# Batch 0's experts chosen in pieces one half of the attention earlier, the last batch's logits and positions moved forward, two batches' shared down products moved behind the experts

## The chip, the core and the metric

The kernel runs on one core of a Trainium2 chip. The metric is the time of one execution in microseconds on the device, as the median of several runs. Engines: PE is TensorE (matmuls; PEld its weight loads), DVE is VectorE, ACT is ScalarE, POOL is GpSimd, SP is SyncE, which here only issues transfers. Each engine runs its own program in order; they wait for each other on semaphores.

## What is computed

One transformer block on x of shape (4, 512, 256): four batches of 512 tokens, model width 256.

```
mod = silu(c) @ wmod -> sa, ca, ga, sb, cb, gb           (per batch; |ga|, |gb| kept >= 0.25)
h   = layernorm(x) * (1 + ca) + sa
att = causal softmax attention(h): 32 query heads, 8 key/value heads, head width 8
x   = x + ga * (att @ wo)
h   = layernorm(x) * (1 + cb) + sb
scores = softmax(h @ gate_w.T)                            (16 experts, 4 groups of 4)
keep the 2 groups with the largest score, then the 4 largest experts in them;
w = their scores, normalised to sum 1
out = sum over experts e of w[e] * (swiglu(h @ expert_up_w[e].T) @ expert_down_w[e].T)
    + swiglu(h @ shared_up_w.T) @ shared_down_w.T
x   = x + gb * out
```

The experts' inner width is 176, that of the shared expert 352.

## The kernel before, in words

**Attention.** It is done in eight halves (u = 0 to 7): batch u // 2, and one half of the heads. A half goes through 10 groups n, each a pair (quarter q of 128 queries, tile kt of 128 keys), and each group through four steps g. A step does one score product into one bank of PSUM (L692, `scores`), which ScalarE exponentiates (L1138); on the diagonal GpSimd masks the result (L1264). Two groups later TensorE multiplies by the values (L703, `weigh_values`), and ScalarE takes the sums out of PSUM (L1119). Meanwhile TensorE computes the scores of the next half a first time, to find the row maxima: 22 pairs of banks in a half (L670, L673, `scores_for_max`), which VectorE reduces (L1456); two pairs of banks exist, so pair n waits for VectorE to be done with pair n - 2. The maxima are transposed (`turn_max`). In the even halves the projection of the batch before (L723, `project`) stands in group 9, and VectorE adds it to x. The score pairs of half 0 are computed before the halves begin (L849), between the projections of q, k and v.

**Bank 7.** The small products of the attention (turned maxima, projections, turned rows, logits, positions) share bank 7; a table, `misc_use` (L290 to L308), numbers them in order, and each waits until the one before is read out.

**The experts' routing,** once for each batch m. VectorE normalises the rows (stats, mean, `centre`) and scales them (`scale_rows`); TensorE transposes them (`turn_first_rows` for batch 0, `turn_rows2` otherwise) and multiplies by the gate (L792, `logits`); VectorE takes the largest logit (L1555) and subtracts it (`begin`); ScalarE exponentiates (`exponential`); VectorE chooses groups and experts (`choose`), some twenty small instructions; TensorE counts, for every row and expert, how many rows come before it (L806 to L812, `positions`); VectorE turns these into slots (`place`, L1594 to L1610); and GpSimd scatters the rows to `x_rows` in memory, 16 indirect DMAs for each batch (L1350), each with 128 rows. GpSimd's program is in order too: the masks of half 7 and the scatters share it.

In the kernel before, batch 0 goes through the logits in half 6 (group 7) and through choose and place in half 7, ahead of VectorE's other work there; batch 1 through its logits in group 5 of half 7; logits(2) stands between the last two value products, before positions(1). GpSimd issues four scatters of batch 0 before the last quarter's masks of half 7, and twelve behind them.

**After attention** come, on TensorE, the shared expert's up products (L879, three parts k for each batch) and down products (L900, two parts h for each batch), the last projection (L916, `project_last`), and between them the routing of batches 2 and 3. Before place(3) SP can't write the 16 pads (L561), which fill the last tile of every expert; behind them it loads the rows tile by tile (L565). The down products of batches 0 to 2 are taken out by ScalarE (L1178) and written to `y_sum[0]`.

**The experts.** 79 tiles of 128 rows: transposed (L953), up (L965), down (L987, L992), weighed by VectorE (L1756), and added into `y_sum` in memory by GpSimd's indirect DMA (L1391). Behind the last tile TensorE computes the down product of batch 3 (L900), which VectorE multiplies by gb and adds to x (L1776, L1779). VectorE adds all parts (L1786 to L1791) after `y_sum` is read back, and the result is written.

The order of the products after attention:

```
shared_up(0, 0); shared_up(0, 1); positions(2); shared_up(0, 2); shared_up(1, 0); shared_up(1, 1)
project_last(0); project_last(1); shared_up(1, 2); shared_up(2, 0); turn_rows2(3)
shared_up(2, 1); logits(3); shared_down(0, 0); shared_down(0, 1); positions(3)
shared_up(2, 2); shared_down(1, 0); shared_down(1, 1); shared_up(3, 0..2); shared_down(2, 0..1)
```

## Time and profile before

| | |
|---|---|
| median of 3 runs | 697.05 us (695.75, 697.05, 705.97) |
| the profiled execution | 700.47 us, of which the span is 698.6 us |
| PE busy | 601.9 us, 86% |
| DVE busy | 403.8 us, 58% |
| ACT busy | 304.6 us, 44% |
| POOL busy | 344.9 us, 49% |
| mean granted clock of TensorE | 0.917 |

The profile comes from one execution. Its span goes from the first to the last recorded instruction; all times in the text are microseconds from its start. Busy time is the time in which at least one instruction of an engine runs; the granted clock is that of TensorE, 1.00 being 2.4 GHz. Half 0 begins at about 72 us, half 7 ends at about 346, the experts run from about 466 to 668.

### The profile page before, as it was taken

What the parts mean: (1) busy time and instruction counts of PE and PEld (TensorE: products, weight loads), DVE (VectorE), ACT (ScalarE), POOL (GpSimd) and SP (SyncE); (2) the same over time, 40 slices, a digit from 0 to 9 for tenths busy, and PEclk for the clock granted to TensorE, in tenths of its full rate; (3) what the DMA queues carried; (4) which work ended last, traced back from release to release, by engine and by line L of the source; (5) the groups of instructions that cost most, each with busy time, mean ns of one, the idle gap of its engine ahead of it and who ended that gap; (6) DMA issues with size and microseconds to landing.
All of it is one profiled execution on the core that took longest, in us unless ns stands there. A gap on an engine that the chain in (4) does not pass through costs nothing.

```text
span 698.6 us, 11637 instructions
## 1 busy us (share of the span) xinstructions
PE 601.9 (86%) x3377; PEld 323.7 (46%) x3377; DVE 403.8 (58%) x819; ACT 304.6 (44%) x626; POOL 344.9 (49%) x451
## 2 busy tenths in 40 slices
PE   7988799999999999998949539939999999999950
PEld 5455433344434443443324116616666666666530
DVE  5668577877898789868744056503333333333327
ACT  2424577776677677757610033113232323323200
POOL 5017745362637273625757702703666666666630
PEclk7989799999999999989969759969999999999975
DMA  9698569674141414201339902544676777777567
GB/s 277 163 274 171 172 138 336 159 218 107 36 107 37 106 37 106 39 17 19 119 95 380 352 37 82 208 127 96 123 124 122 124 130 125 119 127 128 77 124 276
DMA packets 86180, 98.01 MB, mean 140 GB/s; under 512 B 12868, under 2 KB 78964, under 8 KB 85864
## 3 DMA queue, kind: packets, MB, share of 16 engines
q1 hardware_dynamic: 70040, 75.90, 39.2%
q0 software_dynamic: 14448, 19.80, 15.9%
q10 hardware_dynamic: 1632, 1.57, 0.7%
q8 instruction: 30, 0.49, 0.3%
q14 instruction: 30, 0.25, 0.1%
HBM read 50.55 MB, written 43.65 MB: 135 GB/s over the span
## 4 chain that ended last, share of the span: by engine, by line
PE 46%; DMA 18%; issue 11%; DVE 7%; ACT 7%; POOL 5%; SPq 4%; another core or an unknown queue 3%; POOLq 0%; ACTq 0%; DVEq 0%
DMA y_sum<-arena 13%; PE bank L703 9%; PE bank L692 9%; PE bank L965 6%; PE bank L670 4%; ACT arena L1138 4%; PE bank L673 3%; PE bank L987 2%; POOL arena L1264 2%; PE bank L723 2%; ACT arena L1119 2%; PE bank L992 2%; DMA arena<-x_rows 1%; PE bank L623 1%
## 5 line engine op out<-in xcount | busy, mean ns | idle before, releaser
L1456 DVE TENSOR_REDUCE negm<-bank 128x2 f32<-128x1024 f32 (+3 forms) x176 | 192.6, 1121 | 54.9 <-PE bank L673 53.6
L1138 ACT ACTIVATE arena<-bank 128x512 f32<-128x512 f32 x320 | 181.1, 600 | 81.0 <-PE bank L692 74.3
L1391 POOL DMA_INDIRECT y_sum<-arena x79 | 123.1, 1558 | 96.5 <-DVE arena L1756 47.9
L1264 POOL TENSOR_SCALAR_AFFINE_SELECT arena<-arena 128x512 f32<-128x512 f32 x128 | 81.0, 647 | 119.7 <-ACT arena L1138 117.0
L692 PE MATMUL bank<-arena 75*128 75x512 bf16 x320 | 119.6, 394 | 8.8 <-ACT arena L1138 3.0
L965 PE MATMUL bank<-arena 128*128 x316 | 105.9, 478 | 0.6 <-ACT arena L1206 0.3
L1350 POOL DMA_INDIRECT x_rows<-arena,slots x64 | 64.3, 1004 | 55.0 <-DVE slots L1610 36.5
L703 PE MATMUL bank<-arena 128*9 128x512 f32 x640 | 85.6, 607 | 5.3 <-POOL arena L1264 4.1
L1756 DVE TENSOR_SCALAR arena<-bank,arena 128x256 f32<-128x256 f32 x79 | 38.2, 484 | 84.9 <-DMA y_sum<-arena 34.3
L673 PE MATMUL bank<-arena 118*128 118x128 bf16 x512 | 83.8, 228 | 2.4 <-DMA arena<-k_rows 2.4
L670 PE MATMUL bank<-arena 72*128 72x128 bf16 (+2 forms) x384 | 83.4, 279 | 2.6 <-DVE negm L1456 2.6
L1212 ACT ACTIVATE arena<-bank 128x176 f32<-128x176 f32 x79 | 25.1, 318 | 127.3 <-PE bank L965 83.3
L692 PEld LDWEIGHTS bank<-arena 75*128 75x128 bf16 x320 | 30.4, 99 | 98.5 <-ACT arena L1138 82.4
L965 PEld LDWEIGHTS bank<-arena 128*128 128x128 f32 x316 | 57.7, 192 | 39.5 <-issue 15.2
L673 PEld LDWEIGHTS bank<-arena 118*128 118x128 bf16 x512 | 48.2, 102 | 20.5 <-issue 3.6
L879 PE MATMUL bank<-arena 128*128 128x512 f32 (+1 forms) x96 | 49.6, 661 | 8.9 <-issue 8.9
L1748 DVE TENSOR_TENSOR arena<-bank,arena 128x128 f32<-128x128 f32 x79 | 23.1, 292 | 57.3 <-ACT arena L1212 54.3
L670 PEld LDWEIGHTS bank<-arena 72*128 72x128 bf16 x384 | 38.4, 100 | 27.3 <-DVE negm L1456 16.8
L987 PE MATMUL bank<-arena 128*128 x158 | 41.5, 385 | 3.1 <-DVE arena L1756 1.7
L953 PE MATMUL bank<-ident,arena 128*128 128x128 f32 x158 | 25.4, 278 | 13.0 <-DMA arena<-x_rows 12.9
L879 PEld LDWEIGHTS bank<-arena 128*128 128x128 f32 (+1 forms) x96 | 19.0, 202 | 33.9 <-issue 33.8
L1206 ACT ACTIVATE arena<-bank 128x256 f32<-128x256 f32 x79 | 26.6, 382 | 11.2 <-PE bank L953 11.1
(190 smaller groups left out, 704.5 us busy)
## 6 DMA issues: line engine op xcount, KB each, us to landing
arena<-x_rows SPq DMA_DIRECT2D x79, 144.0 KB, 2.5
arena<-q_rows SPq DMA_DIRECT2D x8, 1200.0 KB, 9.2
q_rows<-arena SPq DMA_DIRECT2D x24, 384.0 KB, 4.4
arena<-up_t SPq DMA_DIRECT2D x2, 2816.0 KB
arena<-y_sum SPq DMA_DIRECT2D x8, 512.0 KB, 6.7
x_rows<-arena SPq DMA_DIRECT2D x17, 144.0 KB
k_rows<-arena SPq DMA_DIRECT2D x24, 96.0 KB, 3.2
arena<-k_rows SPq DMA_DIRECT2D x8, 288.0 KB
```

The source lines that it names most:

```text
L670: nc.tensor.matmul(bank[:, buf + j, at_:at_ + n - P], Q[k][0:PR, head, q * P:q * P + P], K[k][0:PR, head // REP, 0:n - P], start=(c == 0), ...
L673: last = nc.tensor.matmul(bank[:, buf + j, at_ + n - P:at_ + n], Q[k][0:MR, head, q * P:q * P + P], K[k][0:MR, head // REP, q * P:q * P + ...
L692: nc.tensor.matmul(bank[:, score_bank(u, tile), :], K[k][0:KR, g, kt * P:kt * P + P], Q[k][0:KR, g * REP:g * REP + REP, q * P:q * P + P], ...
L703: last = nc.tensor.matmul(bank[32 * g:32 * g + VW, OBANK, :], V[:, b * QT + kt, h * GH + g, :], probs[:, (NG * u + n) % SLOTS, g, :], star ...
L879: last = nc.tensor.matmul(bank[0:w, 2 * k + i, :], ws_up[:, c, c0:c0 + w], h2T[n][:, c, :], start=(c == 0), stop=(c == DC - 1))
L965: last = nc.tensor.matmul(bank[:, 2 + t % 2, 0:2 * I], xT[t % 2][:, c, :], w[:, bass.ds(e * (DC * 2 * I) + c * 2 * I, 2 * I)], start=(c == ...
L987: nc.tensor.matmul(bank[:, 6 + i, 0:D], actT[p % 2][:, i, :], main[:, bass.ds(expert[2 * p + i] * D, D)], start=True, stop=False, skip_gro ...
L1138: nc.scalar.activation(probs[:, group % SLOTS, g, :], bank[:, score_bank(u, tile), :], ACT.Exp, scale=SCALE).then_inc(s["st_free"], 1)
L1264: nc.gpsimd.affine_select(out=block_, in_=block_, compare_op=ALU.is_ge, fill=0.0, base=0, pattern=[[0, REP], [1, P]], channel_multiplier=- ...
L1350: gp.indirect_dma_start(x_rows, bass.IndirectOffsetOnAxis(ap=slots[:, t, k:k + 1], axis=0), rows[:, t, :], None).then_inc(s["rows_out"], 16)
L1391: gp.indirect_dma_start(y_sum[t % 2], bass.IndirectOffsetOnAxis(ap=xt[t % XT][:, D:D + 1].bitcast(U32), axis=0), yo[t % YO], None, compute ...
L1456: nc.vector.tensor_reduce(to, view, AX.X, ALU.max, negate=True).then_inc(s["s_free"], 1)
```

## The change

**First half.** Ten products of the identity with itself, whose result nobody reads, stand before half 0, and two more before each of the last four score pairs of half 0. On GpSimd low(3), a small step of the projections, moves from behind the first quarter of half 0 to behind the second.

**Half 6.** The transposes of batch 0 move from groups 4 and 5 to group 2, logits(0) from group 7 to group 4. choose(0) is cut into six pieces, which stand between VectorE's maxima in groups 5 to 7; positions(0) and place(0) follow in group 8. scale_rows(1) moves out of half 6 to the place that choose(0) had in half 7.

**Half 7.** turn_rows2(1) stands in group 1 (was 0), logits(1) in group 3 (was 5), turn_rows2(2) in group 5 (was 7), logits(2) in group 7 (was between the last two value products). GpSimd issues three scatters of batch 0 before the first masks, one behind the second quarter, four behind the third, and the other eight behind the last.

**After attention.** shared_up(2, 1) is cut in two, and logits(3) stands between the parts. positions(3) stands before all four down products of batches 0 and 1 and no longer waits for the first one's eviction. The down products of batch 2 stand behind the experts, with those of batch 3, in banks 0 to 3; VectorE adds both batches' to x, and only batches 0 and 1 go to `y_sum[0]`, which is zeroed for two batches instead of one.

The diff, cut to its core:

```diff
-AMID = 4
+AHEAD, AMID = 3, {1: 1, 2: 4}
...
-                    if u == HALVES - 2 and q == QT - 2:
+                    if u == HALVES - 2 and q == 1:
                         for c in range(DC):
                             misc_use["rows", c] = len(misc_use)
+                    if u == HALVES - 2 and q == 2:
+                        misc_use["logits", 0] = len(misc_use)
...
+        CHOOSE_AT = {(5, 2): 0, (6, 0): 1, (6, 3): 2, (7, 1): 3, (7, 2): 4, (7, 3): 5}
...
-                        sp.dma_start(y_sum[0][(B - 1) * T:NT * P, :].rearrange("(t p) d -> p t d", p=P),
-                                     zeros[:, 0:QT, :]).then_inc(s["y_zero"], 16)
+                        sp.dma_start(y_sum[0][(B - 2) * T:NT * P, :].rearrange("(t p) d -> p t d", p=P),
+                                     zeros[:, 0:2 * QT, :]).then_inc(s["y_zero"], 16)
...
+                    for j in range(idle):
+                        nc.tensor.matmul(bank[:, buf, 0:P], ident[:, :], ident[:, :], start=True, stop=True,
+                                         skip_group_check=True)
...
                             if u == HALVES - 2:
-                                if (n, g) in ((4, 1), (5, 1)):
-                                    turn_first_rows(n - 4)
+                                if (n, g) in ((2, 0), (2, 3)):
+                                    turn_first_rows(g // 3)
+                                if (n, g) == (4, 1):
+                                    logits(0)
+                                if (n, g) == (8, 1):
+                                    positions(0)
+                            if u == HALVES - 1:
+                                if (n, g) == (1, 1):
+                                    turn_rows2(1)
+                                if (n, g) == (3, 1):
+                                    logits(1)
+                                if (n, g) == (5, 1):
+                                    turn_rows2(2)
                                 if (n, g) == (7, 1):
-                                    logits(0)
-                            if u == HALVES - 1:
-                                if (n, g) == (0, 3):
-                                    turn_rows2(1)
-                                if (n, g) == (3, 3):
-                                    positions(0)
-                                if (n, g) == (5, 1):
-                                    logits(1)
-                                if (n, g) == (7, 1):
-                                    turn_rows2(2)
+                                    logits(2)
...
-                        pe.wait_ge(s["ys_ready"], 2)
...
-                        scores_for_max(0, q, i)
+                        scores_for_max(0, q, i, 2 if pair > 17 else 0)
...
+                for i in range(10):
+                    nc.tensor.matmul(bank[:, 3, 0:P], ident[:, :], ident[:, :], start=True, stop=True)
...
                 weigh_values(HALVES - 1, 8)
-                logits(2)
                 weigh_values(HALVES - 1, 9)
                 positions(1)
...
-                    if n == B - 1:
+                    if n == 2:
                         pe.wait_ge(s["xT_ready"], TILES)
+                    if n == 3:
+                        pe.wait_ge(s["a_ready"], TILES)
+                    k_ = 7 - h if n < 2 else 2 * (n - 2) + h
...
-                shared_up(2, 1)
+                shared_up(2, 1, range(1))
                 logits(B - 1)
-                shared_down(0, 0)
-                shared_down(0, 1)
+                shared_up(2, 1, range(1, 2))
+                shared_up(2, 2)
                 positions(B - 1)
-                shared_up(2, 2)
-                shared_down(1, 0)
-                shared_down(1, 1)
+                for n in range(2):
+                    for h in range(2):
+                        shared_down(n, h)
                 for k in range(3):
                     shared_up(3, k)
-                for h in range(2):
-                    shared_down(2, h)
...
-                for h in range(2):
-                    shared_down(B - 1, h)
+                for n in range(2, B):
+                    for h in range(2):
+                        shared_down(n, h)
...
+                EXPONENTIAL_AT = [(HALVES - 2, 5, 0), (HALVES - 1, 4, 3), (HALVES - 1, 9, 1)]
...
+                exponential(B - 1)
                 shared_silu(2, 1)
-                exponential(B - 1)
+                shared_silu(2, 2)
                 store(0)
-                shared_silu(2, 2)
                 store(1)
                 for k in range(3):
                     shared_silu(3, k)
-                store(2)
...
                 for u in range(HALVES):
+                    if u == HALVES - 1:
+                        gp.wait_ge(s["numbered"], 4)
+                        gp.wait_ge(s["routed"], 1)
+                        for k in range(AHEAD):
+                            scatter_first()
...
-                        if (u, q) == (0, 0):
+                        if (u, q) == (0, 1):
                             low(3)
...
-                        if u == HALVES - 1 and q == 2:
+                        if u == HALVES - 1 and q == 1:
                             inverse_deviation(B - 2)
-                            gp.wait_ge(s["numbered"], 4)
-                            gp.wait_ge(s["routed"], 1)
-                            for k in range(AMID):
-                                scatter(0, k)
+                        if u == HALVES - 1 and q in AMID:
+                            for k in range(AMID[q]):
+                                scatter_first()
...
+                            if u == HALVES - 2:
+                                if (n, g) == (4, 3):
+                                    dve.wait_ge(s["numbered"], 4)
+                                    begin(0)
+                                if (n, g) in CHOOSE_AT:
+                                    CHOICE[CHOOSE_AT[n, g]](0)
+                                if (n, g) == (8, 3):
+                                    place(0)
...
                 take_max(u, QT - 1)
-                choose(0)
+                for i in range(QT):
+                    scale_rows(dve, 1, i)
                 for i in range(QT):
                     norm_stats(dve, 2, i)
                 norm_mean(dve, 2)
                 turned_rows(1)
-                place(0)
...
+                for n in range(2, B):
+                    for h in range(2):
+                        g2 = gate_bc[:, n, 1, :].unsqueeze(1).to_broadcast([P, 2, D])
+                        x_h = X[:, n * QT + 2 * h:n * QT + 2 * h + 2, :]
...
+                        dve.wait_ge(s["sh_down"], v + 1)
+                        nc.vector.tensor_tensor(y_shared[:, h], bank[:, v - 4, :].rearrange("p (t d) -> p t d", t=2), g2,
+                                                ALU.mult).then_inc(s["ys_last"], 1)
+                        dve.wait_ge(s["ys_last"], 2 * (v - 4) + 1)
+                        nc.vector.tensor_tensor(x_h, x_h, y_shared[:, h], ALU.add).then_inc(s["ys_last"], 1)
```

## Rows read from the trace of the kernel before

**Rows 1.** The head of the profile page.

```profile
span 698.6 us, 11637 instructions
```

**Rows 2.** Table of stretches (attention, between, experts); columns in its head line.

```profile
core 0: us, PE busy (x) PEld busy (x) DVE busy (x) ACT busy (x) POOL busy (x), PEclk, DMA share, GB/s
72.00:346.00 274.00, 261.73 (x1880) 110.84 (x1881) 220.89 (x329) 193.77 (x355) 140.12 (x269) 0.97 0.42 110
346.00:466.00 120.00, 76.48 (x259) 42.00 (x258) 46.20 (x140) 19.99 (x31) 55.96 (x56) 0.79 0.54 185
466.00:668.00 202.00, 195.79 (x908) 128.25 (x907) 69.52 (x236) 63.21 (x198) 119.43 (x77) 0.98 0.66 116
```

**Rows 3.** Timeline, end of half 7: start, us, engine, line, tile, count [idle before <-releaser].

```profile
338.50 2.41 POOL L1264 TENSOR_SCALAR_AFFINE_SELECT arena<-arena 128x512 f32<-128x512 f32 x4
...
347.55 1.04 PE L703 MATMUL bank<-arena 128*9 128x512 f32 x8
...
355.03 0.96 POOL L1350 DMA_INDIRECT x_rows<-arena,slots  x1 [0.30 <-issue]
358.24 0.23 DVE L1555 TENSOR_REDUCE few<-bank 128x4 f32<-128x64 f32 x1 [10.96 <-remote]
358.34 0.60 ACT L1119 ACTIVATE arena<-bank 128x512 f32<-128x512 f32 x1 [12.15 <-remote]
...
361.14 0.96 POOL L1350 DMA_INDIRECT x_rows<-arena,slots  x1 [5.14 <-DVE slots L1610]
```

**Rows 4.** Timeline, the last projection and the last of 32 scatters.

```profile
380.88 3.72 PE L916 MATMUL bank<-wo_sb,arena 128*128 128x256 f32 x16 [1.58 <-issue]
...
400.97 0.96 POOL L1350 DMA_INDIRECT x_rows<-arena,slots  x1 [0.30 <-issue]
...
406.54 0.69 DVE L1617 TENSOR_TENSOR arena<-bank,gate_bc 128x512 f32<-128x512 f32 x1 [3.63 <-remote]
```

**Rows 5.** Three groups of half 0 and of half 4: line L1138 alone.

```profile
core 0: us, ACT busy (x), PEclk, DMA share, GB/s
74.97:87.92 12.95, 6.92 (x13) 0.77 0.73 232
211.35:221.98 10.63, 6.92 (x14) 1.00 0.21 32
```

**Rows 6.** Stretches of choose(0) and place(0) in half 7; columns as rows 2.

```profile
320.37:327.69 7.32, 5.89 (x41) 1.71 (x39) 6.66 (x32) 6.29 (x14) 5.83 (x11) 1.00 0.12 16
330.63:332.16 1.53, 0.91 (x10) 0.15 (x8) 1.39 (x7) 1.53 (x4) 1.32 (x3) 1.00 0.07 16
```

**Rows 7.** Half 4, its groups 5-9; half 6, its groups 5-9; cold stretch. Columns as rows 2.

```profile
208.22:243.03 34.81, 33.16 (x248) 14.13 (x245) 28.80 (x34) 24.29 (x45) 16.19 (x32) 1.00 0.33 72
225.47:243.03 17.56, 17.05 (x113) 7.20 (x113) 13.94 (x16) 11.80 (x22) 3.92 (x9) 1.00 0.46 106
277.09:316.19 39.10, 38.33 (x272) 17.39 (x269) 29.55 (x36) 25.60 (x48) 15.87 (x32) 0.91 0.12 25
294.05:316.19 22.14, 21.98 (x134) 10.08 (x133) 14.48 (x18) 13.07 (x25) 3.90 (x8) 0.85 0.06 15
306.10:313.00 6.90, 6.90 (x29) 1.76 (x22) 3.94 (x6) 2.90 (x6) 0.00 (x0) 0.51 0.00 0
```

**Rows 8.** Timeline of the last batch's routing, the pads and the first load.

```profile
416.66 4.66 PE L879 MATMUL bank<-arena 128*128 128x512 f32 x8
...
421.15 1.85 PE L792 MATMUL bank<-gate_sb,arena 128*128 128x16 f32 x16
...
429.84 0.19 PE L806 MATMUL bank<-sel_bf,before_bf 128*128 128x64 bf16 x1 [0.78 <-ACT arena L1178]
...
432.15 27.88 SPq L561 DMA_DIRECT2D x_rows<-arena  x16
...
462.26 0.37 SPq L565 DMA_DIRECT2D arena<-x_rows  x1
```

**Rows 9.** Timeline behind the experts: shared down, last add, first final sum.

```profile
667.80 7.20 PE L900 MATMUL bank<-arena 128*128 128x256 f32 x24
...
675.84 0.69 DVE L1779 TENSOR_TENSOR X<-X,arena 128x512 f32<-128x512 f32 x1
...
680.69 1.22 DVE L1786 TENSOR_TENSOR arena<-arena 128x1024 f32<-128x1024 f32 x1 [4.16 <-DMA arena<-y_sum]
```

95 lines of the change are left out of this document (54 added, 41 removed).

## The prediction, made before the changed kernel ran

> **What bounds the kernel now.** I read the page first, for the span of the profiled execution, 698.6 us [rows 1]; it stands 1.55 us above the median of the runs (697.05), so a difference worked out against it is carried over to the median. Then the table of stretches [rows 2]: attention (halves 0 to 7) has TensorE busy for 262 of 274 us, the experts for 196 of 202 us, but the 120 us between them for 76, at a mean clock of 0.79. The change touches all three; its room is in the middle one. I then followed the chain of work that ended last through that stretch, and checked each step in the timeline, taking the consumers' start for the moment at which TensorE's work was really there.
>
> That last point decides the argument. The trace puts the last value product of half 7 (L703) at 347.55 to 348.59, yet ScalarE's L1119, which waits for it, starts at 358.34, and VectorE's begin(2) (L1555), which waits for the logits just before it, at 358.24. Both name a "remote" releaser. GpSimd runs twelve scatters in a row meanwhile, the last from 355.03 to 355.99 [rows 3]. The same comes again: L916, the attention's last projection, stands at 380.88 to 384.60, but VectorE's L1617, which reads it, starts at 406.54, while GpSimd runs 32 scatters from 361.14 to 401.93 [rows 3, 4]. So in both places what TensorE hands on arrives only when a long row of scatters has ended: 2.3 us after in the first, 4.6 after in the second. I call this a hold. Why it happens no row tells.
>
> **The change, part by part.** All times are those of before; I name shifts.
>
> *First half.* Ten idle products stand ahead of half 0 and two in each of the last four score pairs, all in places where TensorE waits for VectorE; low(3) on GpSimd moves behind the next quarter's masks. The stretch of three groups (the twelve exponentials after the first group; the edges are counted too) takes 12.95 us at a clock of 0.77, against 10.63 us in half 4 at 1.00 [rows 5]. If the clock stays at its upper level, 2.4 GHz, and the masks come in time, the difference is got back: **-2.3 us**. Bounds: 0 if the clock falls all the same; -3.5 if the first group, wholly cold now, gains 1.2 beside the 0.77 a group of the other three.
>
> *Half 6.* Choosing and placing batch 0 held VectorE from 320.37 to 327.69 and from 330.63 to 332.16 in half 7, together 8.85 us, taken as 8.8 us of work [rows 6]. It goes into groups 5 to 8 of half 6 in pieces. A steady half (4) takes 34.81 us; its groups 5 to 9 take 17.56 us with 13.94 us of VectorE [rows 7]. With 8.8 more VectorE has 22.8 us of work there: it becomes the bound, since each score pair has but two banks and TensorE waits for the maxima. Between 22.8 (no gap at all) and 26.4 (all of the 3.6 us of gaps of before kept) I take 24, near the packed end, since pairs are buffered two deep. The first five groups of the steady half are 17.25 us, and the logits, moved to group 4, are 16 products of 1.85 us by L792 [rows 8], of which I take 1.5 as added. 17.25 + 1.5 + 24 = 42.8, against 39.10 us now, where half 6 already loses to its logits and to 6.9 us at a clock of 0.51 [rows 7]: **+3.6 us**, bounds +2.4 and +6.1. scale_rows(1), which leaves half 6, lay under TensorE's work and gives nothing; nor do the first rows' transposes, moved three groups.
>
> *Half 7.* VectorE is rid of 8.8 us and takes scale_rows(1). Logits(1), the transposes of batch 2 and logits(2) come two groups and more earlier; logits(2) leaves the place between the last two value products. What is queued behind each wait: behind turn_rows2(1) and logits(1) all of TensorE, behind begin(1) the rest of VectorE's routing; with nothing of batch 0 ahead of them I take these as met. GpSimd issues three scatters before the first masks of half 7, where it was idle, one after the second quarter, four after the third; I take these as hidden. Then eight are left after the last masks instead of twelve. The last masks (L1264, 338.50 to 340.91), now behind four scatters, no longer stand behind them at the end and are done at about 338.5; eight scatters at 1.27 us (0.96 and the 0.30 ahead of it [rows 3], rounded up) end at 348.7. With the same 2.3 us behind the last, the hold ends at 351.0 instead of 358.3: **-7.3 us**. Bounds: -9.7 if TensorE is not held at all (348.6), -0.9 if the hold doesn't follow the scatters. Everything behind L1119 moves with it: the store of the values, the weight loads that SP queues behind them, place(1) and the 32 scatters that follow it with no gap, so also the end of the second hold at 406.54.
>
> *Last batch.* Behind the transposes (L780) half of a shared up product stands before the logits instead of a whole one. L879 took 416.66 to 421.32 partly at the lower clock; its first half would end at 419.5, so logits start 1.8 us earlier. Then positions(3) (L806) waited 0.78 us for an eviction of the first batch's down products; now it stands before them [rows 8]. **-2.6 us**; bounds -0.8, and -3.1 with half of the 4.66 us for the first. It carries over whole, since after place(3) SP writes 16 pads (L561, 432.15 to 460.03) before it loads the first expert rows (L565, 462.26) [rows 8]: that train starts when place(3) is done, and nothing else is later. The last 16 scatters need 16 x 1.27 = 20.3 us beside it and are hidden, and so are the down products; the two batches' that leave save nothing here for that reason. Behind the moved down products stand gated(2) and tables() on VectorE; they are due before the pads' end, and VectorE is busy for only 46 of the 120 us [rows 2], so I take them as met.
>
> *Tail.* Two batches' down products now stand behind the experts, 48 records instead of 24. The 24 take 7.20 us, partly cold; two sets of 12 more at 2.6 us warm end at 680.2 instead of 675.0. VectorE's last multiply and add (0.69 us each, L1779) then end at 681.6, where the final sums (L1786) now start at 680.69 [rows 9]: **+0.9 us**, with 4.3 of the 5.2 us hidden under the read of y_sum. Bound +8 if all 48 run at the lower clock, 0 below. The zeros written for one batch more lie in attention at a DMA share of 0.42 [rows 2]: nothing.
>
> Sum: -2.3 + 3.6 - 7.3 - 2.6 + 0.9 = -7.7. The profiled execution would be 690.9 us, the median 697.05 - 7.7 = **689.3 us**.
>
> One page speaks against the largest term. The Trainium skill, "SBUF — State Buffer", section "Who interferes with whom", has it that DMA never contends with a compute engine and that TensorE and ScalarE wait for nobody. Rows 3 and 4 don't agree with that reading of scatters beside TensorE: the signals are 10 and 22 us late. By that rule the sum would be that of the first rival.
>
> **The rivals.**
>
> *The hold doesn't follow the scatters.* TensorE was not held while four scatters ran in half 7, nor in the first 9 us of the 32; another cause, such as the traffic of that moment, would stay where it is. Then the third term is -0.9 and the sum -1.3: 695.7 us. Against it: the two holds end with the two rows of scatters.
>
> *The clock falls in half 6.* VectorE-bound pieces leave TensorE with gaps all through groups 5 to 9, and these rows show what that can lead to: around the present logits 6.9 us ran at 0.51, and groups 5 to 9 took 22.14 us instead of 17.56 [rows 7]. Of those 4.6 us, 1.5 are the logits, so a cold stretch of 6.9 us costs 3.1. If 20 us are cold, that is three such stretches, +9.3: the sum is +1.6, 698.6 us, slower than before. It decides if more than 17 us of half 6 run at the lower clock (7.7 / 3.1 x 6.9).
>
> *The projection gets ahead of the second hold.* If enough products are through before the hold closes, VectorE has L1617 as soon as the reciprocals allow, near 385 instead of 406.5; that is 15 to 20 us more, about 672 us. Against it: the 32 scatters start at once after place(1) as now.
>
> **How the numbers follow.** The forecast 0.53, the hold elsewhere 0.20, the cold half 0.15, the projection ahead 0.12. The range goes from 682 (the lower bounds -3.5, +2.4, -9.7, -3.1 and 0 sum to -13.9: 683.1, and a little room) to 699 (the cold half, 698.6) and leaves out only the projection ahead and what lies beyond the slow case. Two per cent, about what a measurement of this kernel can tell from no change, is 683.1 and 711.0 us. Faster than that: the projection ahead, and a little of the forecast, 0.13. Slower: none of the cases, but a cold half with a cold tail would come near, 0.04. Within: 0.83.
>
> **What the profile after would show.** The three groups of half 0 in 10.6 us at a clock near 1. Half 6 at 42.8 us, with VectorE busy over 22 of 24 us in groups 5 to 9. Batch 0's last scatter near 348.7 and L1119 about 2.3 us behind it, in times shifted by +1.3. L1617 7.3 us nearer to the start of half 7's end than now, and the first load of expert rows 30.1 us after the first pad, as now [rows 8]. The final sums' start set by VectorE, not by the load of y_sum. I am wrong if L1119 starts more than 5 us after the last scatter of batch 0, if half 6 takes over 45 us, or if the pads' train no longer sets the start of the experts.

## The result and the profile after

The changed kernel takes 702.2 us in the median of 19 runs, the kernel before 697.1 in 19 runs beside them: a ratio of 1.0074, with a 95% interval of 1.0055 to 1.0093. Forecast were 689.3 us, faster by 1.1%, and a range up to 699; it came out slower by 0.7%. Every ratio in this text leaves out the executions that took over 1.5% longer than the fastest of their kernel. Three later comparisons of the same two kernels gave 1.0018 (0.9973 to 1.0063), 0.9981 (0.9949 to 1.0013) and 1.0011 (0.9978 to 1.0044). So the loss is between nothing and 0.9%, and in none of the four was there the forecast gain.

The line numbers of the changed kernel are other ones: L1154 is the exponential (L1138 before), L1278 the mask (L1264), L1132 takes the values out (L1119), L711 is the value product (L703), L1364 the scatter (L1350), L930 the last projection (L916), L1668 the addition that reads it (L1617), L802 the logits (L792), L815 the positions (L806), L914 the shared down product (L900), L565 the pads (L561), L569 the load of rows (L565).

The head of the page after, for [rows 1]:

```profile
span 701.5 us, 11712 instructions
```

The table of stretches after, columns as in [rows 2]: half 6, half 7, and in them a stretch at the upper and one at the lower clock:

```profile
275.13:317.95 42.82, 39.38 (x280) 17.27 (x277) 34.31 (x68) 25.74 (x48) 16.33 (x33) 0.92 0.11 23
317.95:357.23 39.28, 35.97 (x187) 14.30 (x185) 22.78 (x66) 23.43 (x47) 28.12 (x36) 0.78 0.24 73
314.90:328.60 13.70, 11.45 (x66) 5.73 (x67) 12.76 (x28) 6.41 (x12) 10.17 (x13) 1.00 0.09 35
328.60:345.60 17.00, 16.52 (x63) 7.02 (x61) 7.13 (x21) 8.08 (x17) 10.59 (x14) 0.50 0.35 96
```

Half 6 takes 42.82 us, to the tenth what was forecast, though with 6.8 us of it at the lower clock, which the forecast had not counted. But half 7 takes 39.28 where it took 29.39, and 17 us of it run at a granted clock of 0.50. Ahead of that stretch VectorE was busy for 12.76 of 13.70 us and TensorE for 11.45.

The timeline after at the end of half 7, for [rows 3]: last masks, last exponential, last value product, last scatter of batch 0, values out, place(1), the next scatter.

```profile
348.06 1.81 POOL L1278 TENSOR_SCALAR_AFFINE_SELECT arena<-arena 128x512 f32<-128x512 f32 x3 [0.24 <-ACT arena L1154]
...
357.23 0.60 ACT L1154 ACTIVATE arena<-bank 128x512 f32<-128x512 f32 x1 [0.17 <-remote]
...
357.88 1.04 PE L711 MATMUL bank<-arena 128*9 128x512 f32 x8 [1.58 <-issue]
...
358.93 0.96 POOL L1364 DMA_INDIRECT x_rows<-arena,slots  x1 [0.31 <-issue]
...
361.59 0.60 ACT L1132 ACTIVATE arena<-bank 128x512 f32<-128x512 f32 x1 [3.76 <-remote]
361.68 0.23 DVE L1651 TENSOR_TENSOR rt<-bank,taken 128x64 f32<-128x64 f32 x1 [9.93 <-remote]
...
363.51 0.96 POOL L1364 DMA_INDIRECT x_rows<-arena,slots  x1 [3.62 <-DVE slots L1661]
```

The hold ends 1.7 us behind the last scatter (358.93 + 0.96), which the forecast had nearly right (2.3). But the scatters end at 359.9 and not at 348.7 (350.0 with the forecast's own shift of +1.3 up to half 7), since the last masks were done at 349.87 and not at 338.5 (339.8 with the shift).

The second hold and the last batch, for [rows 4] and [rows 8]:

```profile
380.76 3.62 PE L930 MATMUL bank<-wo_sb,arena 128*128 128x256 f32 x16
...
392.74 0.69 DVE L1668 TENSOR_TENSOR arena<-bank,gate_bc 128x512 f32<-128x512 f32 x1 [7.87 <-remote]
...
403.38 0.96 POOL L1364 DMA_INDIRECT x_rows<-arena,slots  x1 [0.30 <-issue]
...
408.93 0.69 DVE L1668 TENSOR_TENSOR arena<-bank,gate_bc 128x512 f32<-128x512 f32 x1 [14.78 <-remote]
...
420.87 1.85 PE L802 MATMUL bank<-gate_sb,arena 128*128 128x16 f32 x16
...
428.72 0.20 PE L815 MATMUL bank<-sel_bf,before_bf 128*128 128x64 bf16 x1 [0.75 <-DVE sel_bf L1624]
428.95 10.62 PE L914 MATMUL bank<-arena 128*128 128x256 f32 x48
...
431.57 32.49 SPq L565 DMA_DIRECT2D x_rows<-arena  x16
...
466.28 1.49 SPq L569 DMA_DIRECT2D arena<-x_rows  x2
```

The first half of the projection got through early (392.74), the second half again 4.6 us behind the last scatter. The pads' train starts 0.6 us earlier than before (431.57 against 432.15), but takes 32.49 instead of 27.88 us.

Behind the experts, for [rows 9]:

```profile
669.48 12.52 PE L914 MATMUL bank<-arena 128*128 128x256 f32 x48
...
682.84 0.69 DVE L1835 TENSOR_TENSOR X<-X,arena 128x512 f32<-128x512 f32 x1
683.56 1.22 DVE L1842 TENSOR_TENSOR arena<-arena 128x1024 f32<-128x1024 f32 x1
```

The ledger between the two profiled executions, after less before, each line from the same two events in both traces:

| from | to | forecast | measured |
|---|---|---|---|
| start | end of half 5 | -2.3 | -1.96 |
| | end of half 6 | +3.6 | +3.72 |
| | last exponential of half 7 | 0 | +9.89 |
| | values out (L1119) | -7.3 | -8.40 |
| | first pad | -2.6 | -3.83 |
| | first load of expert rows | 0 | +4.60 |
| | last scatter-add | 0 | -1.94 |
| | final sums, end | +0.9 | +0.80 |
| sum | | -7.7 | +2.88 |

### The profile page after: what moved, and what is told of

Its sections match the earlier page's. It is cut to its first block, busy times and chain, and to the rows that moved or that the text cites. A ratio compares the mean times of both kernels' runs of the same rounds, so it can differ in the third digit from the quotient of the medians.

```text
span 701.5 us, 11712 instructions
## 1 busy us (share of the span) xinstructions
PE 606.4 (86%) x3413; PEld 327.5 (47%) x3413; DVE 406.2 (58%) x823; ACT 303.1 (43%) x624; POOL 346.0 (49%) x451
## 4 chain that ended last, share of the span: by engine, by line
PE 61%; DVE 9%; SPq 7%; issue 6%; ACT 5%; DMA 5%; POOL 4%; another core or an unknown queue 3%; DVEq 0%; POOLq 0%; ACTq 0%
PE bank L977 15%; PE bank L711 8%; PE bank L700 8%; PE bank L999 5%; PE bank L1004 4%; PE bank L678 3%; ACT arena L1154 3%; PE bank L965 2%; PE bank L889 2%; POOL arena L1278 2%; PE bank L681 2%; PE bank L914 2%; DVE negm L1483 2%; SPq L564 2%
## 5 line engine op out<-in xcount | busy, mean ns | idle before, releaser
L1154 ACT ACTIVATE arena<-bank 128x512 f32<-128x512 f32 x320 | 181.1, 599 | 92.8 <-PE bank L700 84.7
L1278 POOL TENSOR_SCALAR_AFFINE_SELECT arena<-arena 128x512 f32<-128x512 f32 x128 | 83.0, 664 | 112.0 <-ACT arena L1154 109.4
L711 PE MATMUL bank<-arena 128*9 128x512 f32 x640 | 87.9, 622 | 6.5 <-ACT arena L1154 2.3
L1364 POOL DMA_INDIRECT x_rows<-arena,slots x64 | 63.6, 993 | 59.3 <-DVE slots L1661 41.0
L681 PE MATMUL bank<-arena 118*128 118x128 bf16 x512 | 82.2, 223 | 3.8 <-DMA arena<-k_rows 2.8
L889 PE MATMUL bank<-arena 128*128 128x512 f32 (+1 forms) x96 | 45.7, 632 | 0.0
L965 PEld LDWEIGHTS bank<-ident,arena 128*128 128x128 f32 x158 | 19.9, 143 | 31.0 <-issue 26.1
```

What stands on the lines that cost most here:

```text
L681: last = nc.tensor.matmul(bank[:, buf + j, at_ + n - P:at_ + n], Q[k][0:MR, head, q * P:q * P + P], K[k][0:MR, head // REP, q * P:q * P + ...
L711: last = nc.tensor.matmul(bank[32 * g:32 * g + VW, OBANK, :], V[:, b * QT + kt, h * GH + g, :], probs[:, (NG * u + n) % SLOTS, g, :], star ...
L889: last = nc.tensor.matmul(bank[0:w, 2 * k + i, :], ws_up[:, c, c0:c0 + w], h2T[n][:, c, :], start=(c == 0), stop=(c == DC - 1))
L1154: nc.scalar.activation(probs[:, group % SLOTS, g, :], bank[:, score_bank(u, tile), :], ACT.Exp, scale=SCALE).then_inc(s["st_free"], 1)
L1278: nc.gpsimd.affine_select(out=block_, in_=block_, compare_op=ALU.is_ge, fill=0.0, base=0, pattern=[[0, REP], [1, P]], channel_multiplier=- ...
L1364: gp.indirect_dma_start(x_rows, bass.IndirectOffsetOnAxis(ap=slots[:, t, k:k + 1], axis=0), rows[:, t, :], None).then_inc(s["rows_out"], 16)
```

## The experiments

Kernels told of together ran on one chip, with runs of the kernel before beside them; between such groups only ratios are compared. "Behind half 5" is L1119's counterpart less half 5's last exponential, the stretch on which the forecast's two largest terms lie.

**The parts one by one.** Each is the kernel before with one group of the diff's lines.

*First half alone:*

```diff
+                        scores_for_max(0, q, i, 2 if pair > 17 else 0)
...
+                for i in range(10):
+                    nc.tensor.matmul(bank[:, 3, 0:P], ident[:, :], ident[:, :], start=True, stop=True)
...
+                        if (u, q) == (0, 1):
                             low(3)
```

> The kernel before with the first-half part of the change alone (idle products ahead of half 0 and in its last four score pairs, low(3) behind the second quarter). Half 0 was 34.51 us before and 31.54 in the changed kernel, half 1 32.66 and 33.41. Theory A (this part works by itself and is worth what the ledger shows up to the end of half 5): halves 0 to 5 together 2.0 us shorter than before, the time 2.0 us below it, since nothing behind it is moved. Rival B (the tail of the clock's pattern moves with it and takes it back): halves 0 to 5 shorter by 2.0 us, but one of the later low stretches moves into half 6 or 7 and the time is within 1 us of before.

Ratio 0.9987 (0.9951 to 1.0024), which tells neither theory from the other. Half 0 31.54 us instead of 34.51, half 1 33.43 instead of 32.66, halves 0 to 5 together 2.4 us shorter. The second row below is half 6, with the code of before:

```profile
72.00:82.00 10.00, 8.76 (x79) 4.44 (x79) 7.32 (x9) 7.22 (x14) 9.39 (x18) 1.00 0.79 247
272.82:309.26 36.44, 35.31 (x272) 16.79 (x269) 29.38 (x36) 25.61 (x49) 16.19 (x32) 1.00 0.12 27
```

Half 0 now runs at full clock. And half 6 takes 36.44 us, not the 39.11 of [rows 7]: the cold stretch there, one at the lower clock, came with that execution, not with the code.

*Halves 6 and 7 alone* (all lines of the diff that name HALVES - 1 or HALVES - 2, CHOOSE_AT, CHOICE, AHEAD and AMID):

> The kernel before with the part in halves 6 and 7 alone (batch 0 chosen in pieces and placed in half 6, its scatters spread over half 7, the other logits earlier). Theory A (VectorE-bound groups at the end of half 6 leave TensorE with gaps, the clock falls in half 7 and costs about 8 of its 9.9 us): half 6 3.7 us and half 7 8 to 10 us longer than before, at least 14 us of half 7 at a granted clock of 0.50, batch 0's last scatter near 362, and the time 4 to 7 us above before. Rival B (the loss of the changed kernel comes mostly from behind attention, where the pads' train took 32.49 us instead of 27.88): half 7 as long, but hidden by the hold that ends earlier, and the time within 2 us of before.

Ratio 0.9970 (0.9928 to 1.0012): the expected loss of 4 to 7 us did not show; the time is about where Rival B had it, within 2 us of before. Half 6 42.60 us, half 7 37.39 with 10.3 us at the lower clock (14 were expected), 83.88 us behind half 5. Its profiled execution, 704.11 us, is 6 us above its median of 698.01; the rows of one execution and the median of ten are not the same thing here.

*The last batch alone* (shared_up cut, positions(3) first, down products of batch 2 behind the experts):

> The kernel before with the part behind attention alone (half of an up product moved behind logits(3), positions(3) ahead of all down products, the down products of batch 2 behind the experts). Theory A (this part loses: with 48 down products in a row the stretch in which signals come late is longer, and SyncE's pads with it): positions(3) 1.1 to 2.6 us earlier, the pads' train about 32 instead of 28 us, the first load of expert rows 2 to 4 us later, the final sums 0.8 us later relative to the last scatter; time 2 to 4 us above before. Rival B (the longer train comes only from where attention ended in the changed kernel): the train 28 us as before, the first load 2 us earlier and the time 1 to 2 us below before.

Ratio 1.0039 (1.0004 to 1.0074). Logits to positions 7.85 us instead of 8.69; the train 31.32 us, while in the two kernels beside it without this part it took 27.64 each; final sums 9.6 us behind the last scatter-add instead of 9.0. Theory A. The rows of last_batch_only:

```profile
428.64 31.32 SPq L561 DMA_DIRECT2D x_rows<-arena  x16
```

and of first_half_only:

```profile
425.84 27.64 SPq L561 DMA_DIRECT2D x_rows<-arena  x16
```

**Is it the clock?**

```diff
-                                    scores_for_max(u + 1, q, i)
+                                    scores_for_max(u + 1, q, i, 2 if u == HALVES - 2 and q == QT - 1 else 0)
...
+                    for i in range(2 if u == HALVES - 1 and n < 4 else 0):
+                        nc.tensor.matmul(bank[:, score_bank(u, tile), 0:P], ident[:, :], ident[:, :], start=True,
+                                         stop=True, skip_group_check=True)
```

> The changed kernel with two idle products more in each of half 6's last-quarter score pairs and ahead of each score product of the first four groups of half 7, so that TensorE stays busier where it waited for VectorE; nothing else is changed. Theory A (the clock is the cause of half 7's length): the 17.1 us at 0.50 from 328.6 on shrink to less than 7, half 7 goes from 39.3 to about 32 to 34 us and the time 4 to 7 us below that of the changed kernel, near 697. Rival B (the scatters ahead of the masks and the work put ahead on VectorE are the cause): the clock stays up but half 7 stays above 37 us, and the time within 2 us of the changed kernel or above it.

Ratio 1.0056 (1.0020 to 1.0092).

```profile
317.59:355.08 37.49, 35.84 (x255) 19.91 (x252) 22.46 (x66) 23.87 (x47) 25.57 (x35) 1.00 0.25 72
```

The clock stayed up, and half 7 is still 37.49 us. But the test was spoiled: the idle products take 0.61 us by their rows for each of 16 score products, and the product behind them starts 0.45 us after they do, so 7.2 to 9.8 us in all that TensorE did not have. Without them the half would be 27.7 to 30.3 us, an estimate. Only groups 4 to 9, without them, can be read: 17.0 us against 20.3 in the changed kernel, where their first 8.6 us are cold.

**What makes half 7 long?** The changed kernel again, for a reference on the same chip:

> The changed kernel again, unchanged, on the chip and beside the runs on which the following kernels stand. Theory A (the sum of its parts is what it costs: the halves part moves the end of the first hold 5 us later against a kernel with a full clock in half 6, the last batch's part adds 3.5 us, the first half gives 2 back): time 4 to 7 us above the kernel before. Rival B (the three parts measured alone, -0.9, -2.1 and +2.7 per thousand-odd, simply add up): within 2 us of before.

1.0018, as Rival B had it; half 7 38.02 us, 17.1 of them at the lower clock. Beside it, first, the scatters back where they were (AHEAD 0, AMID four behind the third quarter):

```diff
-AHEAD, AMID = 3, {1: 1, 2: 4}
+AHEAD, AMID = 0, {2: 4}
```

> The changed kernel with GpSimd's scatters of batch 0 where the kernel before had them (none ahead of half 7's masks, four behind the third quarter, twelve behind the last). Theory A (the scatters among the masks make half 7 long): half 7 goes from 39.3 us to 35 or less, but the last scatter comes four scatters (5.1 us) later relative to the end of the masks and the first hold ends at about the same time, so the time is within 2 us of the changed kernel. Rival B (the products and the clock make it long, the scatters don't): half 7 within 1.5 us of the changed kernel's at an equal clock, the first hold ends 3 to 5 us later, and the time is 3 to 5 us above the changed kernel.

Ratio 0.9935 (0.9880 to 0.9989), but it rests on the five shortest of ten times; the median of all ten, 697.73 us, is 0.2% above the kernel before (696.03). This is no gain that can be relied on. Half 7 32.16 us, with 3.4 cold, and L1119's counterpart comes in the middle of the row of scatters, which ends at 361.7:

```profile
355.70 0.96 POOL L1364 DMA_INDIRECT x_rows<-arena,slots  x1 [0.30 <-issue]
356.78 0.60 ACT L1132 ACTIVATE arena<-bank 128x512 f32<-128x512 f32 x1 [4.04 <-remote]
```

Neither theory had that: half 7 was shorter as A said, but the hold ended before the scatters did. And the shorter half is not the work of the scatters' place. A later profile of the changed kernel (whole_fourth) has as little cold time, 3.4 us, with the scatters among the masks, and its half 7 is as short; the first row is that one, the second whole_again:

```profile
316.86:349.29 32.43, 29.70 (x187) 11.56 (x185) 22.82 (x66) 23.08 (x47) 26.90 (x34) 0.95 0.27 79
316.41:354.43 38.02, 35.77 (x187) 14.34 (x185) 22.68 (x66) 23.19 (x48) 27.19 (x35) 0.78 0.23 71
```

The ten times fall in two groups, four of 687.7 to 691.2 us and six of 696 to 704.4; in the profiled one, of the low group, both halves of the projection were through by 393.3 (410.35 in the changed kernel).

Second, scale_rows(1) back in half 6, in the places it had:

```diff
-                            if u == 4 and (n, g) in SCALE_AT:
-                                scale_rows(dve, 0, SCALE_AT[n, g])
+                            if u in (4, 6) and (n, g) in SCALE_AT:
+                                scale_rows(dve, u // 2 - 2, SCALE_AT[n, g])
...
-                for i in range(QT):
-                    scale_rows(dve, 1, i)
```

> The changed kernel with scale_rows(1) back in half 6, spread over its first groups as in the kernel before, and not ahead of VectorE's work in half 7. Theory A (VectorE's long instructions beside GpSimd's masks at the start of half 7 make both slow and bring the second quarter's masks 1.4 us late relative to the half's start): groups 0 to 2 of half 7 go from 12.2 us to about 10.8, as before, half 7 1.5 us shorter. Rival B (the delay comes from the end of half 6 alone): groups 0 to 2 stay at 12 us. The time by A 1 to 2 us, by B not below the changed kernel.

Ratio 0.9901 (0.9855 to 0.9947), 5.7 us below whole_again, where Theory A had 1 to 2. Half 7, and its groups 0 to 2:

```profile
317.79:347.89 30.10, 27.87 (x187) 11.42 (x185) 21.43 (x62) 23.12 (x47) 25.37 (x34) 1.00 0.29 85
317.79:328.57 10.78, 9.21 (x56) 3.84 (x54) 9.38 (x19) 7.36 (x16) 9.54 (x16) 1.00 0.16 49
```

Groups 0 to 2 take 10.78 us, as expected, against 12.18 in the changed kernel, and the cold stretch is gone. Where the 1.4 us are lost stands in the timeline of the changed kernel:

```profile
322.14 1.65 DVE L355 SCALAR_TENSOR_TENSOR arena<-arena,norm_rs,gate_bc 128x256 f32<-128x256 f32 x4
...
322.27 2.61 POOL L1278 TENSOR_SCALAR_AFFINE_SELECT arena<-arena 128x512 f32<-128x512 f32 x2 [0.27 <-ACT arena L1154]
...
326.54 3.72 POOL L1278 TENSOR_SCALAR_AFFINE_SELECT arena<-arena 128x512 f32<-128x512 f32 x5
326.61 3.16 DVE L346 SCALAR_TENSOR_TENSOR arena<-X,norm_mv,gate_bc 128x256 f32<-128x256 f32 x4
...
330.36 1.90 PE L711 MATMUL bank<-arena 128*9 128x512 f32 x8 [0.48 <-POOL arena L1278]
```

and in that of after_scale_in_half_6:

```profile
322.10 1.23 POOL L1278 TENSOR_SCALAR_AFFINE_SELECT arena<-arena 128x512 f32<-128x512 f32 x2 [0.27 <-ACT arena L1154]
...
324.97 3.54 POOL L1278 TENSOR_SCALAR_AFFINE_SELECT arena<-arena 128x512 f32<-128x512 f32 x5
```

Beside scale_rows (L355) two masks take 2.61 us instead of 1.23; it is one of them that lasts 2.02 us instead of 0.63, while the four L355, at 0.47 us each, are not slowed. The second quarter's masks then start 8.59 us into the half instead of 7.18, and TensorE's value products wait for masks. Elsewhere VectorE pays too: four L346 beside masks take 3.16 us, 1.67 where there are none, and that in both kernels. The Trainium skill, "SBUF — State Buffer", section "Who interferes with whom", states that a VectorE instruction with two inputs in SBUF contends with a GpSimd instruction that reads SBUF. These rows agree. The price is not the same each time: one mask three times as long beside L355, and beside L346 the masks 1.3 times (0.82 us) and VectorE 1.8 times (0.85 us).

**Does the hold follow the scatters?** The kernel before, with the row in another order:

```diff
-                for m in range(B):
+                for m in (1, 2, 0, 3):
```

> The kernel before with batch 0's last twelve scatters issued behind those of batch 2 and no longer behind half 7's last masks; their number is the same. Theory A (TensorE's signals come late while a long row of scatters runs, so the hold follows the scatters): L1119, 12.8 us behind the last exponential of half 7, comes less than 3 us behind it; the row of scatters that follows is 44 long and starts 9 us earlier, so it ends 5 to 7 us later than now, and what waits for the last projection with it, unless the projection gets through; the time 4 to 7 us above before. Rival B (the hold has another cause): L1119 stays 12 to 13 us behind half 7's last exponential and the second hold ends as early as now.

Ratio 1.0104 (1.0028 to 1.0179), from four executions.

```profile
347.59 1.04 PE L703 MATMUL bank<-arena 128*9 128x512 f32 x8
348.71 0.60 ACT L1119 ACTIVATE arena<-bank 128x512 f32<-128x512 f32 x1 [2.71 <-PE bank L703]
...
350.80 0.98 POOL L1350 DMA_INDIRECT x_rows<-arena,slots  x1 [12.06 <-DVE slots L1610]
```

The first hold is gone: L1119 stands at 348.71, 3.3 us behind the last exponential instead of 12.8, with the same products on TensorE. The row of 44 scatters ends at 406.9 (401.9 before), the last addition at 414.4 (409.4), the logits 5.3 us later. That is Theory A, or within 0.4 us of it at each point. But the first half of the projection came at 399.57, 7.3 us before the row of 44 ended, so not every signal waits for the end of a row; and 6.8 us of half 7 ran cold here (31.37 us), so its code of before isn't free of that either.

**The combinations,** four kernels on one chip. Down products spread:

```diff
-                for n in range(2):
-                    for h in range(2):
-                        shared_down(n, h)
-                for k in range(3):
-                    shared_up(3, k)
+                shared_down(0, 0)
+                shared_down(0, 1)
+                shared_up(3, 0)
+                shared_down(1, 0)
+                shared_up(3, 1)
+                shared_down(1, 1)
+                shared_up(3, 2)
```

> The changed kernel with scale_rows(1) back in half 6, as in after_scale_in_half_6, and with the down products of batches 0 and 1 spread between the up products of batch 3 (two, up, one, up, one, up) and not four in a row; nothing is left out. Theory A (the row of 48 short products beside the last 16 scatters is what makes the pads' train 31 to 32.5 us instead of 28): the train 28 to 29 us, the first load of expert rows 29.5 to 31 us behind the first pad, the time 2 to 4 us below after_scale_in_half_6's. Rival B (any dense stretch of TensorE's does it): the train stays at 31 to 32 us and the time within 1.5 us of it.

The last batch's part left out:

> The changed kernel with scale_rows(1) back in half 6 and with everything behind attention as in the kernel before (order of the shared products, logits(3), positions(3), one batch's down products behind the experts). Theory A (the last part costs 3 to 4 us in the train and 0.8 us at the end, and gives back 1 to 1.5): the train 28 us, the final sums' start no later than 8.9 us behind the last scatter-add, the time 2 to 3 us below after_scale_in_half_6. Rival B (the last part is worth its move): time 1 us or more above after_scale_in_half_6.

The scatters as before:

> The changed kernel with scale_rows(1) back in half 6 and with the scatters of batch 0 where the kernel before had them. Theory A (with scale_rows out of the way the spread scatters are what ends the first hold early): L1119's counterpart no more than 5 us behind half 7's last exponential, but the row of 32 scatters begins 4 to 6 us later than in after_scale_in_half_6 because twelve are left, and the time is 2 to 5 us above it. Rival B (the scatters' place is worth nothing): half 7 within 1 us of 30.1, the time within 1.5 us of after_scale_in_half_6.

Scatters and logits(2) as before, scale_rows(1) not:

> The changed kernel with the scatters of batch 0 and logits(2) both where the kernel before had them. Between half 7's last exponential and L1119's counterpart there were 12.8 us in the kernel before (twelve scatters behind the masks, logits(2) between the last value products), 3.3 without the twelve scatters and 4.6 with them but logits(2) earlier. Theory A (the first hold needs both, the row of scatters and the burst of short logits products in it): about 12.8 us again, and 2.3 us behind the last scatter. Rival B (the hold of the kernel before came from something else that the change moved): below 6 us.

On this chip the kernel before took 656.0 us, not 697. The ratios are 1.0018 (0.9989 to 1.0048), 1.0051 (1.0019 to 1.0083), 1.0084 (1.0050 to 1.0119), and the last took 669.4 in its one run. Rows of scale6_downs_spread:

```profile
348.98 1.04 PE L711 MATMUL bank<-arena 128*9 128x512 f32 x8 [0.41 <-ACT arena L1156]
...
349.93 0.96 POOL L1366 DMA_INDIRECT x_rows<-arena,slots  x1 [0.30 <-issue]
350.10 0.60 ACT L1134 ACTIVATE arena<-bank 128x512 f32<-128x512 f32 x1 [1.17 <-PE bank L711]
...
367.89 3.62 PE L930 MATMUL bank<-wo_sb,arena 128*128 128x256 f32 x16
...
369.81 0.69 DVE L1670 TENSOR_TENSOR arena<-bank,gate_bc 128x512 f32<-128x512 f32 x1 [0.41 <-PE bank L930]
```

There is no hold in any of the four: L1119's counterpart comes 1.8 to 3.3 us behind the last exponential, with scatters on both sides, and the train takes 21.2 to 22.7 us. So a hold is not what scatters do by themselves, and the fourth kernel could not answer its question here. The second kernel's half 7 (29.98 us) and the third's (34.14, 10.3 of them cold) give the price of the cold: groups 3 to 5 of the third take 13.38 us at a clock of 0.62, those of after_scale_in_half_6 9.76 at 1.00. It also shows again that the scatters' place does not set the half's length: 34.14 us here, and 34.15 with them spread in scale6_second below, both with 10.2 us cold. The third against the first (scatters moved, and the down products spread) is 0.7%, the second against the first (the last batch's part, spread) 0.3%.

**Another chip with holds.** The kernel before for its rows, then three more:

> The kernel before, unchanged, for its rows on the same chip as the three that follow. Theory A (the holds come with the chip, not with the kernel): beside a kernel before near 656 us L1119 stands less than 4 us behind half 7's last exponential and L1617 within 25 us of it; beside one near 697 us 12 to 13 and about 61 us. Rival B (the holds were taken away by what the last four kernels changed): 12 to 13 us whatever the time.

695.4 us. L1119 12.6 us behind the last exponential, 2.2 behind the last scatter; L1617 at 403.33, 4.7 behind the last of the 32: the holds of [rows 3, 4] again. So Theory A: on the five chips of these experiments the holds came and went with the chip. A chip's state at the time can't be told from the chip itself here, since each was used once, and the kernel before has a time but no profile on the chip without holds. Half 6 here:

```profile
278.27:314.38 36.11, 35.32 (x272) 16.80 (x269) 29.56 (x36) 25.61 (x49) 15.82 (x32) 1.00 0.12 27
```

> The changed kernel, unchanged. Theory A (the halves part moves the end of half 7 some 14 us later against a kernel with half 6 at a full clock, of which the end of the first hold gives back 9 where there is one and nothing where there is none): on a chip without holds the time is 8 to 12 us above the kernel before (about 1.5 per cent); on one with holds 1 to 5 us above. Rival B (what lies behind attention takes up a later end of half 7 on any chip): within 3 us of the kernel before.

0.9981, within 3 us as Rival B had it; half 7 35.71 us, 10.2 cold; 83.6 us behind half 5, which is 5.6 more than in before_again (78.0).

> The changed kernel with scale_rows(1) back in half 6 (as after_scale_in_half_6). Theory A: half 7 about 30 us again, 8 us shorter than with the whole change, at a full clock, and the time 5 to 8 us below whole_third. Rival B (that kernel's half 7 was short by luck of the clock): at least 10 us of half 7 at the lower clock and the time within 3 us of whole_third.

0.9951 (0.9908 to 0.9994). Half 7 34.15 us, 10.2 us of it cold: groups 0 to 2 are short again (10.8), but the cold stretch came back. That is Rival B: by the ratio it stands 0.3% below whole_third, by the medians (694.4 and 694.1 us) not at all.

> The kernel before with the first half's part and the last batch's part of the change, the down products of batches 0 and 1 spread between batch 3's up products, and without the part in halves 6 and 7. Theory A (the halves part is what costs, the other two give 2 to 4 us): time 2 to 4 us below the kernel before on a chip without holds, within 2 us of it with holds, and below whole_third by 5 us or more. Rival B (the parts' shares of the time are all within the spread): within 2 us of whole_third.

1.0020 (0.9989 to 1.0052): without the halves part nothing was gained either; the train was 30.00 us. By the medians it is 3.3 us above whole_third (697.4 and 694.1), where Theory A had it 5 us below. So the runs don't lay the whole loss on the halves part.

**A last pair:**

> The changed kernel, unchanged. Theory A: beside a kernel before near 656 us (no holds) half 6 and half 7 together 12 to 16 us longer than 65.7 with nothing to give it back, the time 5 to 12 us above before; beside one near 697 us -1 to +5 us. Rival B (what lies behind attention takes a later end of half 7 up): within 3 us of before on either.

1.0011. Half 7 32.43 us, 3.4 cold, and 80.0 us behind half 5.

> The changed kernel with scale_rows(1) back in half 6 and with the down products spread. Theory A (the row of short products lengthens the train): with holds the train 28 to 30 us against 31 in whole_fourth, the time 4 to 8 us below whole_fourth; without holds the train 22 us in both and the time 5 us or more below whole_fourth, by half 7 alone. Rival B (any dense stretch does it): the train as long as whole_fourth's, within 0.5 us.

1.0010 (0.9980 to 1.0041). Half 7 31.40 us at full clock. The train 32.02 us against 31.41: Rival B. It was not the four down products in a row that made it long, and the times don't differ. What a whole change costs where there is no hold was not measured: no run of it fell on such a chip.

## Why the prediction was wrong

**The base of half 6.** The term +3.6 was taken against the 39.11 us of [rows 7], whose cold stretch of 6.9 us the prediction saw and left in. In four other profiles of that code half 6 took 36.1 to 36.4 us at full clock, in a fifth 41.0 with 10.2 cold. And the profiled execution, 700.47 us, lay 3.4 us above the median; the prediction compared its span, 698.6, with the median and so called it 1.55. The 42.8 us came out (42.6 to 42.9 in nine of fourteen profiles of the changed code), but in part by luck: all nine have 6.8 to 10.2 us at the lower clock, which the sum left out. Groups 5 to 9, taken as 24 us, measure 23.9 with 6.8 us cold, 22.5 with 3.4 (scale6_spread_second), and 22.1 with none in after_warm. What the 42.8 cost is 6.4 us, above the forecast's upper bound of 6.1.

**Half 7,** the step that failed. "With nothing of batch 0 ahead of them I take these as met", and the last masks "are done at about 338.5". Nothing was worked out for the rest of the half, and its term in the sum was 0. Measured it is +9.9 us in the profiled execution, +3.0 to +8.6 in the three others of the same kernel. Three things in the half were changed.

(1) scale_rows(1), 1.65 us of VectorE's two-input instructions, was put beside the first masks: 1.4 us, shown by taking it back (12.18 and 10.78; in the second trial 10.78 again). The prediction had written that it "lay under TensorE's work and gives nothing" where it left half 6, and did not price where it went.

(2) The clock: groups 7 to 9 of half 6 and 0 to 2 of half 7 leave TensorE gaps, and 3.4 to 17.1 us of half 7 ran at 0.50 in all seven profiles with scale_rows(1) at its front (after_warm aside), in two of six without, and in two of six with the halves as before (3.4 and 6.8). Its price shows in the four profiles of the changed kernel, where the code is the same: with 3.4 us cold half 7 takes 32.43 us, with 10.2 35.71, with 17.1 38.02 and 39.28. Groups 3 to 5, where most of it lies, take 9.61 us in whole_fourth at full clock and 15.91 in the profiled execution, 8.38 in the kernel before. So some 6.3 of the 9.9 us go with the clock. Why one execution has three times as much cold time as another no row tells. The rival had the mechanism, but in half 6, and priced from 17 us on.

(3) The rest, the scatters among the masks and a second set of logits, is small: with scale_rows(1) away and nothing cold half 7 takes 30.0 to 31.4 us in four profiles, 0.6 to 2.0 more than before.

**The hold's end, -7.3.** Right in kind: twelve scatters taken from behind the masks took the hold away, and in three of four profiles of the changed kernel it ended 1.6 to 1.7 us behind the last one. Counted from the end of half 7 it gave even more than forecast (-8.4). What failed is the point it was counted from: the last masks were done 10.1 us later than assumed, the forecast's shift of +1.3 included. The bound of -0.9, on which the first rival's sum rests, has no working. Together, half 6, half 7 and the hold were forecast at -3.7 us, from half 5's end to L1119. Four profiles of the changed kernel give 80.0 to 86.5 us for it, mean 84.0, five with the halves as before 78.0 to 83.0, mean 79.9: +4.2. That is 7.9 of the 10.6 us by which the sum was off. And the step's assumption, that the hold ends behind the last scatter, is no rule: it ended 4.9 us before the scatters did in after_scatters_as_before, 3.0 before in after_scale_in_half_6, and 1.4 before in whole_fourth.

**Last batch, -2.6.** The start of the pads came as forecast or better: L1119 to the first pad 69.9 to 70.0 us in three of the four profiles and 72.7 in the fourth, 72.5 to 74.5 with the order of before. But that isn't this part's doing alone: by itself (last_batch_only) it made 72.6. Behind the last of the 32 scatters the first pad comes after 30.2 us in both profiles of the kernel before, 29.4 with this part alone, and 27.2 in all four of the changed kernel, where the first half of the projection had got ahead. Only 0.3 us are the positions, since place(3) waited 0.5 longer for VectorE's weights. What failed is "that train starts when place(3) is done, and nothing else is later": its length was taken as fixed, and on chips with holds it is 30.0 to 32.5 us in ten of the eleven profiles with this part (27.8 in after_scatters_as_before), and 26.5 to 27.9 in the five without it. In the profiled execution seven of the sixteen pads, from 438.0 to 456.3, take over half of it. Why the moved products lengthen it stays open; spreading them did not help.

From half 5's end to the first load of expert rows, the three terms together, the forecast was -6.3 us (3.6 - 7.3 - 2.6). The four profiles of the changed kernel give 186.3 to 191.2 us, mean 188.4; three with both parts as before (before, before_again, first_half_only) 179.3 to 185.2, mean 182.5: +5.9 where -6.3 was forecast.

**Right:** the first half (-2.3; -2.0 in the ledger, from a half 0 that gave 3.0 and a half 1 that took 0.8 back), with the clock as its reason: halves 0 to 5 take 202.0 to 204.0 us with nothing cold in the fifteen profiles with this part, 204.4 to 206.2 with 8 to 15 us cold in the five without. Right too are VectorE as the bound of half 6's last groups (busy 21.4 of 23.9 us) and the tail (+0.9; +0.8), set by VectorE's last addition and not by the read; in the other profiles with that part the final sums start 9.1 to 11.5 us behind the last scatter-add, 8.9 to 9.2 without it. Of the rivals, the projection did get ahead: by half in the changed kernel, whole in one trial, and it was worth far less than 15 us, because in that trial, too, logits(3) did not start before 5 us behind the row of scatters. The experts' 2 us are within their spread: from the first load to the last scatter-add the twenty profiles have 206.2 to 211.8 us.

None of the three signs of being wrong that the prediction named showed in the profiled execution: L1119 came 1.7 us behind the last scatter, half 6 took 42.8 us, and the first load came 2.2 us behind the pads' train, as before. None of them looked at half 7.

No version is clearly better than both kernels. The one with scale_rows(1) in half 6 came out at 0.9901 and 0.9951 where there are holds, by the ratio below the changed kernel both times; with the down products spread it was 1.0010 where there are holds and 1.0018 where there are none, so the gain did not come back a third time.

## What to carry to other kernels

When work is moved off a full stretch, price it again where it lands, beside what the other engines run there, and follow the delay to the end of that stretch before anything behind it is moved by a constant. Before a number is taken from one profiled execution, ask whether a cold stretch in it belongs to the kernel or to that execution, and compare execution time with execution time, not a span with a median. A gain that rests on a stall with no cause in the rows is worth a separate chance.

## What the hardware showed that was not expected

One chip ran the kernel before at 656.0 us, the others at 696 to 701. Most of the difference is the holds, as far as the profiles show it: from L1119's counterpart to the last projection's addition 19.7 us there (350.10 to 369.81, in scale6_downs_spread), 48.2 in the kernel before on the first chip, and from there to the first load of expert rows 47.0 against 55.7. During a hold signals of TensorE come late while GpSimd's scatters keep their 1.27 us, and SyncE's train of 16 pads, 21.2 to 22.7 us on that chip, takes 26.5 to 32.5 on the others. Twelve scatters in a row taken away ended a hold, but such a row on that chip made none. The Trainium skill, "NOTIFIC — the notification-queue block", section "3. Interfaces", says that the block which writes the engines' records can hold its producers back when an internal FIFO fills; that would fit records that run ahead of their signals, and no run here shows whether it is so.

Executions of one kernel on one chip spread by 6 to 17 us, and the mean granted clock goes along with it: the two shortest of the changed kernel's 19 (695.6 and 695.8 us) have 0.933, those above 703 us 0.921 to 0.926.
